# A mixture-of-experts kernel: y scatters in pairs, gathers on ACT's queue, 2 KB weight rows, and a plan in three parts

## The chip, the cores and the metric
One core of a Trainium2 chip runs the program. The metric is the device time in microseconds, the median of three runs. The profiled execution is one more run of the same kernel, read from its trace. TensorE is PE in the profile, VectorE DVE, ScalarE ACT, GpSimd POOL, SyncE SP.

## The reference
Float32 throughout; x is (32, 112, 256), the context (32, 375, 192).

```
x = x + xattn(layernorm(x), ctx)              # 8 heads of 64, softmax(q k') v, Wout, bout
x = x + ffn(layernorm(x))

def ffn(x):                                    # 3584 tokens, D 256, H 512, 8 experts, 2 of them per token
    logits = x @ Wr / sqrt(256)
    idx = top_k(logits + rb, 2)
    w = softmax(logits[idx])
    routed = sum over the two: w * (((x @ W1[e]) * silu(x @ W3[e])) @ W2[e])
    shared = ((x @ Ws1) * silu(x @ Ws3)) @ Ws2
    return routed + shared
```

## The kernel before
Matrices are split into a high and a low part, and a product is made from three matmuls, so weights exist as hi and lo halves.

**Attention** (`attention`, up to about 733 us) goes over 16 pairs of batch rows. Beside it the experts' weights are loaded half an expert at a time, split, and written to `wsplit` in DRAM: 16 halves, each `[128, 3072]` floats, so one row of 12 KB for each partition (`store_half`). W3, W1 and W2 with their lo parts make six `PIECES` of 512 columns.

**Experts** (`experts`) is a software pipeline over steps g: 28 shared steps ("S", one tile of 128 tokens each, with weights that lie in SBUF), then 63 routed steps ("R", one block j of 128 rows of one expert each). In step g TensorE does the up matmuls of g (`up3`, `up1`), the transposes of the hidden of g-1 (`turn`), the transposes of block g-26 (`turn_block`) and the down matmuls of g-1 (`down`). ACT does the scaled copy of y of g-2 (`copy_y`, L1238, into one of three `y_sb`), the Silu of g, the high part of the hidden of g-1 and that of block g-26 (`xr_hi`). VectorE does the addition of the shared y of g-2 into `acc` (`add_y`, L1453), the low part of g-1, the product (`hid`), and the low part of the block. Every engine works through its list in order and waits on semaphores.

While the shared steps run, the tokens are routed, in chunks of 512: VectorE finds the two experts, TensorE ranks the tokens in each (L1601 on), and GpSimd scatters each row with its token number and share to `x_sorted_scratch`, sorted by expert. After the last chunk, in step 19, VectorE makes the whole plan in one go (`make_plan`, L1374 to L1407): for each of the 63 blocks its expert, first row, place of its weights in the ring, and which of its rows lie outside. The rest of VectorE's step 20 stands behind it. SP then writes zeros behind each expert's last row (`padded`), for which it needs `row_end` from the plan.

In the routed stage:
- SP fills a ring of three slots with an expert's weights, two DMAs of 1536 KB each (`fill`, L1080). Slot 2 lies over `acc`, so fill 2 waits until all shared results are stored to `z_scratch` in DRAM. Fill e > 2 waits for the last down matmul of expert e-3.
- GpSimd loads block j's rows from `x_sorted_scratch` into one of four `xg` (`gather`, L1177), five blocks ahead, and adds y to its tokens' rows in `z_scratch` with an indirect accumulating DMA (`scatter_y`, L1186). Two experts may add to the same token, and two accumulates of one row must not be in flight together, so scatter j waits until scatter j-1 has landed. Rows outside the expert go to 128 dump rows behind the tokens.
- After the last scatter SP copies `z_scratch` to the output.

Of the kernel before, what the change touches and what calls it, by code (L numbers as in the profile page):

```python
# [10 lines left out]
F32 = mybir.dt.float32  # L11
F32R = mybir.dt.float32r
U32 = mybir.dt.uint32
# [7 lines left out]
def wait(eng, sem, count):  # L21

    if not isinstance(count, int) or count > 0:
        eng.wait_ge(sem, count)
# [110 lines left out]
def build(nc, x, ctx, Wq, Wk, Wv, Wout, bout, Wr, rb, W1, W2, W3, Ws1, Ws2, Ws3, out):  # L135
# [20 lines left out]
    PIECES = 6  # L156
# [9 lines left out]
    z_dram = nc.dram_tensor("z_scratch", (TOKENS + 128, D), F32, kind="Internal").ap()  # L166

# [44 lines left out]
def attention(nc, g):  # L212
# [15 lines left out]
    with own:  # L228
# [117 lines left out]
        def _(sp):  # L346
# [596 lines left out]
def experts(nc, g):  # L943
# [17 lines left out]
    SLOT = PIECES * 1024  # L961
    AHEAD = 5
    ROUND = 12582912.0
# [4 lines left out]
    with own:  # L968
# [35 lines left out]
        most, total, total_inv = sb("most", [128, TC]), sb("total", [128, TC]), sb("total_inv", [128, TC])  # L1004
        euler, dump_p = sb("euler", [128, 2, TC]), sb("dump_p", [128, 1])

# [33 lines left out]
        scattered = [sem(f"scattered{i}") for i in range(3)]  # L1040
        counts_made, plan, plan_ready = sem("counts_made"), sem("plan"), sem("plan_ready")
        chosen_ready, chosen_exp, shares_ready = sem("chosen_ready"), sem("chosen_exp"), sem("shares_ready")
# [6 lines left out]
        xr_made, xr_hi_ready, xr_ready = sem("xr_made"), sem("xr_hi_ready"), sem("xr_ready")  # L1049
        y_out = [sem(f"y_out{i}") for i in range(3)]  # L1050
        ring_in, zero_ready, padded = sem("ring_in"), sem("zero_ready"), sem("padded")
# [16 lines left out]
        def _(sp):  # L1068
# [21 lines left out]
            sp.wait_ge(zero_ready, 1)  # L1090
            sp.dma_start(z_dram[TOKENS:TOKENS + 128, :], zero_row[:, 0:D]).then_inc(z_stored, 16)
# [8 lines left out]
            sp.wait_ge(z_stored, 16 * (CHUNKS + 1))  # L1100
            for e in range(2, E):
# [5 lines left out]
            for i in range(3):  # L1107
                sp.wait_ge(y_out[i], 16 * ((BLOCKS - i + 2) // 3))
            whole = lambda t: t.rearrange("n d -> (n d)").rearrange("(p f) -> p f", p=128)
# [4 lines left out]
        def _(pool):  # L1114
# [7 lines left out]
                      allow_small_or_imprecise_dtypes=True)  # L1122
            pool.iota(dump_p[:], pattern=[[0, 1]], base=TOKENS, channel_multiplier=1,
                      allow_small_or_imprecise_dtypes=True)
# [82 lines left out]
            pool.wait_ge(plan_ready, 1)  # L1207
            pool.wait_ge(padded, 16 * E)
            for i in range(3):
                pool.wait_ge(scattered[i], 16 * 2 * TC * ((CHUNKS + 2 - i) // 3))  # L1210
            for j in range(AHEAD):
                gather(j)
            for j in range(BLOCKS):
                if j + AHEAD < BLOCKS:
                    gather(j + AHEAD)
                scatter_y(j)

        @block.scalar
        def _(act):
# [12 lines left out]
            def copy_y(g):  # L1232

                j = STEPS[g][1]
                act.wait_ge(y_made, g + 1)
                wait(act, y_out[j % 3], 16 * (j // 3))
                act.wait_ge(to_row_ready, j + 1)
                act.activation(y_sb[j % 3], YB[:, 0:D], ACT.Copy, scale=share[:, j:j + 1]).then_inc(y_copied, 1)  # L1238
# [36 lines left out]
            for g in range(LAST + 2):  # L1275
# [7 lines left out]
                if 0 <= j < BLOCKS:  # L1283
                    hi_of_block(j)
                if g < SHARED_FIRST:
                    c, at_step = (g + 2) // 3, g % 3
                    if at_step == 0 and c + 1 < CHUNKS:
                        normed(c + 1)
                    if at_step == 1 and 1 <= c < CHUNKS:
                        hi_of_x(c)  # L1290

        @block.vector
        def _(dve):
# [76 lines left out]

            def make_plan():

                dve.wait_ge(counts_made, 1)
                linked(dve.tensor_copy(count[:], XB[0][:, 0:E]))  # L1374
                linked(dve.tensor_scalar(blocks_f[:], count[:], 1.0 / BLOCK, 0.498, ALU.mult, ALU.add))
                linked(dve.tensor_scalar(blocks_f[:], blocks_f[:], ROUND, None, ALU.add))
# [6 lines left out]
                dve.tensor_copy(table_rows[:, 2, 0:1], count[:, 0:1])  # L1383
                dve.tensor_tensor(table_rows[:, 2, 1:E], count[:, 1:E], count[:, 0:E - 1], ALU.subtract)
# [6 lines left out]
                linked(last)  # L1391
                dve.tensor_reduce(expert1[:], past[:], AX.X, ALU.add)
                for n in range(3):
                    last = dve.tensor_reduce(of_block[:, n, :], past_of[:, n], AX.X, ALU.add)
                linked(last)
                dve.tensor_scalar(last_row[:], blocks_f[:, E - 1:E], float(BLOCK), float((E - 1) * CAP - BLOCK),
                                  ALU.mult, ALU.add)
                dve.tensor_tensor(row_end[:], count[:], base_e[:], ALU.add)
                dve.tensor_scalar(ring_at[:], of_block[:, 0, :], float(SLOT), None, ALU.mult)
# [6 lines left out]
                dve.tensor_scalar(from_row[:], row_f[:], last_row[:, 0:1], None, ALU.min)  # L1406
                dve.tensor_scalar(outside[:], left[:], iota_p[:, 0:1], dump_p[:, 0:1], ALU.is_le,  # L1407
                                  ALU.mult).then_inc(plan_ready, 1)

# [48 lines left out]
            for g in range(LAST + 2):  # L1458
# [10 lines left out]
                if g < SHARED_FIRST:  # L1469
# [193 lines left out]
```

## Time and profile before
| | before |
|---|---|
| median of 3 runs | 1270.85 us (1267.88 to 1272.77) |
| profiled execution, time | 1277.05 us |
| its span | 1275.4 us |
| mean granted TensorE clock | 0.957 |
| TensorE busy | 1165.7 us, 91% |
| VectorE busy | 748.1 us, 59% |
| ScalarE busy | 671.6 us, 53% |
| GpSimd busy | 802.0 us, 63% |

Times in the profile count from the span's start; the granted clock is 1.00 at 2.4 GHz and 0.50 at 1.2 GHz. An engine's busy share is a mean over stages with different limits, so stretches and waits have to be read as well. A timeline row gives start and duration, the engine and line, output<-inputs with their shapes, and in brackets how long the engine was idle before it and on whom it waited.

### The profile page before, as it was taken

What the parts mean: (1) busy time and instruction counts of PE and PEld (TensorE: products, weight loads), DVE (VectorE), ACT (ScalarE), POOL (GpSimd) and SP (SyncE); (2) the same over time, 40 slices, a digit from 0 to 9 for tenths busy, and PEclk for the clock granted to TensorE, in tenths of its full rate; (3) what the DMA queues carried; (4) which work ended last, traced back from release to release, by engine and by line L of the source; (5) the groups of instructions that cost most, each with busy time, mean ns of one, the idle gap of its engine ahead of it and who ended that gap; (6) DMA issues with size and microseconds to landing.
All of it is one profiled execution on the core that took longest, in us unless ns stands there. A gap on an engine that the chain in (4) does not pass through costs nothing. (4 is left out here: it accounts for less than half of the span.)

```text
span 1275.4 us, 27342 instructions
## 1 busy us (share of the span) xinstructions
PE 1165.7 (91%) x7710; PEld 1014.8 (80%) x7710; DVE 748.1 (59%) x2147; ACT 671.6 (53%) x1743; POOL 802.0 (63%) x867
## 2 busy tenths in 40 slices
PE   5989999999999999999998789996989999999792
PEld 4778888888888888888887678885878888888582
DVE  4667787778777877777777456565433333343231
ACT  4667776777677767776775342331233343433240
POOL 4778977897789778977897435654124444443241
PEclk9989999999999999999999689997999999999796
DMA  4213132213221322132214282212163354336634
GB/s 128 82 38 104 51 120 92 96 51 120 92 97 51 120 91 97 51 120 89 99 32 155 79 315 93 104 64 105 50 240 59 55 129 82 56 58 188 196 52 132
DMA packets 77104, 128.47 MB, mean 101 GB/s; under 512 B 18816, under 2 KB 63696, under 8 KB 72880
## 3 DMA queue, kind: packets, MB, share of 16 engines
q1 hardware_dynamic: 62256, 102.80, 23.9%
q0 software_dynamic: 14784, 24.84, 9.7%
q8 instruction: 37, 0.61, 0.2%
q14 instruction: 27, 0.22, 0.1%
HBM read 77.81 MB, written 53.48 MB: 103 GB/s over the span
## 5 line engine op out<-in xcount | busy, mean ns | idle before, releaser
L513 POOL TENSOR_TENSOR probs<-probs,inv_sum 112x375 f32<-112x375 f32 x256 | 208.9, 817 | 97.6 <-DVE inv_sum L742 97.6
L1186 POOL DMA_INDIRECT z_scratch<-stage,to_row x63 | 100.8, 1599 | 202.9 <-DMA z_scratch<-stage,to_row 102.6
L600 ACT ACTIVATE probs<-bank,neg_max 112x375 f32<-112x375 f32 x256 | 147.2, 575 | 126.7 <-DVE neg_max L730 123.5
L1432 DVE TENSOR_TENSOR hT_lo<-bank,hT_hi 128x512 fp32r<-128x512 f32 x91 | 62.9, 691 | 236.9 <-ACT hT_hi L1230 231.0
L730 DVE TENSOR_REDUCE neg_max<-bank 112x1 f32<-112x375 f32 x256 | 127.7, 541 | 32.5 <-PE bank L878 32.1
L907 PE MATMUL bank<-ident,probs 112*125 112x112 f32 x768 | 138.8, 291 | 7.7 <-POOL probs L513 7.7
L757 DVE TENSOR_TENSOR pT_lo<-bank,pT_hi 125x336 fp32r<-125x336 f32 x256 | 129.5, 506 | 27.1 <-ACT pT_hi L615 20.7
L907 PEld LDWEIGHTS bank<-ident,probs 112*125 112x125 f32 x768 | 107.2, 191 | 42.5 <-issue 24.4
L1224 ACT ACTIVATE stage<-bank 128x512 f32<-128x512 f32 x91 | 54.4, 598 | 154.9 <-PE bank L1496 152.7
L479 POOL TENSOR_TENSOR v_lo<-v_raw,v_hi 125x512 fp32r<-125x512 f32 x96 | 123.5, 1287 | 7.5
L615 ACT ACTIVATE pT_hi<-bank 125x336 fp32r<-125x336 f32 x256 | 113.4, 443 | 12.8 <-PE bank L907 12.8
L796 PE MATMUL bank<-pT_hi,v_hi 125*128 125x224 f32 x384 | 110.4, 287 | 2.0 <-DVE pT_lo L757 2.0
L476 POOL TENSOR_TENSOR v_hi<-v_raw,one 125x512 fp32r<-125x512 f32 x96 | 100.1, 1043 | 13.8 <-ACT v_raw L577 13.8
L796 PE MATMUL bank<-pT_hi,v_lo 125*128 125x224 f32 x384 | 106.7, 278 | 0.0
L1494 PE MATMUL bank<-ring,xr_hi 128*128 x252 | 106.3, 422 | 0.1
L796 PE MATMUL bank<-pT_lo,v_hi 125*128 125x224 f32 x384 | 106.1, 276 | 0.0
L1495 PE MATMUL bank<-ring,xr_hi 128*128 x252 | 100.0, 397 | 0.0
L1496 PE MATMUL bank<-ring,xr_lo 128*128 x252 | 100.0, 397 | 0.0
L742 DVE RECIPROCAL inv_sum<-row_sum 112x1 f32<-112x1 f32 x256 | 41.2, 161 | 92.8 <-ACT probs L600 92.7
L1177 POOL DMA_DIRECT2D xg<-x_sorted_scratch x63 | 66.7, 1059 | 33.3 <-issue 33.3
L688 DVE TENSOR_TENSOR k_lo<-bank,k_hi 128x376 fp32r<-128x376 f32 x128 | 69.3, 543 | 24.7 <-ACT k_hi L574 24.7
L1555 PE MATMUL bank<-ring,hT_hi 128*128 x504 | 78.2, 299 | 1.8 <-issue 1.0
(263 smaller groups left out, 3400.6 us busy)
## 6 DMA issues: line engine op xcount, KB each, us to landing
w_split_scratch<-stage SPq DMA_DIRECT2D x16, 1536.0 KB, 5.7
ring<-w_split_scratch SPq DMA_DIRECT2D x16, 1536.0 KB
stage<-in_L_ffn_W SPq DMA_DIRECT2D x48, 256.0 KB, 3.1
ctx_in<-in_ctx SPq DMA_DIRECT2D x32, 281.2 KB
xg<-x_sorted_scratch POOLq DMA_DIRECT2D x63, 136.0 KB, 3.5
x_in<-in_x SPq DMA_DIRECT2D x16, 224.0 KB, 4.0
x_res<-in_x SPq DMA_DIRECT2D x32, 112.0 KB, 3.1
x_scratch<-x SPq DMA_DIRECT2D x32, 112.0 KB, 1.9
```

The lines of the kernel that those rows point to most:

```text
L476: pool.tensor_tensor(v_hi[b][:, t, :], v_raw[at_v][:], one[0:KR, :].to_broadcast([KR, INNER]), ALU.mult).then_inc(v_hi_ready, 1)
L479: pool.tensor_tensor(v_lo[b][:, t, :], v_raw[at_v][:], v_hi[b][:, t, :].bitcast(F32), ALU.subtract).then_inc(v_ready, 1)
L513: pool.tensor_tensor(probs[:, s % 4, :], probs[:, s % 4, :], inv_sum[:, s:s + 1].to_broadcast([N, M]), ALU.mult).then_inc(probs_ready, 1)
L600: act.activation(probs[:, s % 4, :], S_BANK[s % 2][0:N, 0:M], ACT.Exp, bias=neg_max[:, s:s + 1], accum_out=row_sum[:, s:s + 1]).then_inc(e ...
L615: act.activation(pT_hi[:, (t // 2) % 2, :, t % 2, :], PT_BANK[t % 2][0:KR, 0:KT * N].rearrange("p (t n) -> p t n", t=KT), ACT.Copy).then_i ...
L730: dve.tensor_reduce(neg_max[:, s + n:s + n + 1], S_BANK[n][0:N, 0:M], AX.X, ALU.max, negate=True).then_inc(max_ready, 1)
L757: dve.tensor_tensor(pT_lo[:, (t // 2) % 2, :, t % 2, :], PT_BANK[t % 2][0:KR, 0:KT * N].rearrange("p (t n) -> p t n", t=KT), pT_hi[:, (t / ...
L796: mm = pe.matmul(o, lhsT, rhs, start=(n == 0), stop=(n == len(pairs) - 1))
L907: mm = pe.transpose(PT_BANK[t % 2][0:KR, kt * N:(kt + 1) * N], probs[:, t % 4, kt * KR:(kt + 1) * KR], ident[0:N, 0:N])
L1186: pool.indirect_dma_start(out=z_dram[:, :], out_offset=bass.IndirectOffsetOnAxis(ap=to_row[:, j:j + 1], axis=0), in_=y_sb[j % 3], in_offse ...
L1494: pe.matmul(o, hi, whi, start=(k == 0), stop=False)
L1495: pe.matmul(o, hi, wlo, start=False, stop=False)
```

## The change
- **Scatters.** `y_out` has two semaphores by turns. Scatter j waits for scatter j-2, and for j-1 only where j is the first block of an expert: the plan holds in `must_land[j]` to what value the other semaphore must have come. Two blocks in flight use different sets of dump rows (256 in all). There are four `y_sb`.
- **Gathers.** They move from GpSimd's queue to ACT's, four blocks ahead: gather j stands at the end of ACT's step j+24, behind `xr_hi` of block j-2. What the first gather waits for (the plan, the padding, the scattered rows) moves to ACT with it.
- **Weight rows.** `wsplit` becomes `(16, 6, 128, 512)`: stores and fills move 768 rows of 2 KB each in place of 128 of 12 KB.
- **Plan.** `make_plan` of step 19 becomes `plan_experts` (step 20, ending the wait of SP's padding early through `ends_ready`), `plan_blocks` (step 21), and `plan_sums` with `plan_rows` (step 22). `plan_rows` has two operations more, for `must_land`. Fill 2 waits for the plan as well.

```
-    wsplit = nc.dram_tensor("w_split_scratch", (HALVES, 128, 3072), F32, kind="Internal").ap()
+    wsplit = nc.dram_tensor("w_split_scratch", (HALVES, PIECES, 128, 512), F32, kind="Internal").ap()
...
-                sp.dma_start(wsplit[bass.ds(h, 1), :, :].rearrange("o p n -> p (o n)"),
-                             stage[:, 0:3072]).then_inc(stage_free, 16)
+                sp.dma_start(wsplit[bass.ds(h, 1), :, :, :].rearrange("o m p n -> p (o m) n"),
+                             stage[:, 0:3072].rearrange("p (m n) -> p m n", m=PIECES)).then_inc(stage_free, 16)
...
-    AHEAD = 5
+    AHEAD = 4
...
+        y_sb.append(sb("y_sb3", [128, D])[:])
...
-                    sp.dma_start(ring[:, cols].bitcast(F32), wsplit[2 * e + k]).then_inc(ring_in, 16)
+                    sp.dma_start(ring[:, cols].bitcast(F32).rearrange("p (m n) -> p m n", m=PIECES),
+                                 wsplit[2 * e + k].rearrange("m p n -> p m n")).then_inc(ring_in, 16)
...
-            sp.wait_ge(plan_ready, 1)
+            sp.wait_ge(ends_ready, 1)
             for e in range(E):
                 end = sp.value_load(row_end[0:1, e:e + 1], min_val=0, max_val=E * CAP - BLOCK)
...
-            def gather(j):
-                if j >= 4:
-                    pool.wait_ge(xr_made, j - 3)
-                    pool.wait_ge(to_row_ready, j - 3)
-                row = pool.value_load(from_row[0:1, j:j + 1], min_val=0, max_val=E * CAP - BLOCK)
-                pool.dma_start(xg[j % 4][:], xs_dram[bass.ds(row, BLOCK), :]).then_inc(xg_in[j % 4], 16)
...
             def scatter_y(j):
-                pool.wait_ge(y_copied, j + 1)
+                if 1 <= j < 3:
+                    pool.wait_ge(y_out[(j - 1) % 2], 16)
+                elif j >= 3:
+                    pool.wait_ge(y_out[(j - 1) % 2],
+                                 pool.value_load(must_land[0:1, j:j + 1], min_val=16, max_val=16 * BLOCKS))
+                    pool.sem_inc(landed, 1)
+                if j >= 2:
+                    pool.wait_ge(y_out[j % 2], 16 * (j // 2))
                 if j == 0:
                     pool.wait_ge(z_stored, 16 * (CHUNKS + 1))
-                else:
-                    pool.wait_ge(y_out[(j - 1) % 3], 16 * ((j - 1) // 3 + 1))
+                pool.wait_ge(y_copied, j + 1)
                 pool.indirect_dma_start(
                     out=z_dram[:, :], out_offset=bass.IndirectOffsetOnAxis(ap=to_row[:, j:j + 1], axis=0),
-                    in_=y_sb[j % 3], in_offset=None, compute_op=ALU.add).then_inc(y_out[j % 3], 16)
+                    in_=y_sb[j % 4], in_offset=None, compute_op=ALU.add).then_inc(y_out[j % 2], 16)
...
+            def gather(j):
+                if j == 0:
+                    act.wait_ge(plan_ready, 1)
+                    act.wait_ge(padded, 16 * E)
+                    for i in range(3):
+                        act.wait_ge(scattered[i], 16 * 2 * TC * ((CHUNKS + 2 - i) // 3))
+                if j >= 4:
+                    act.wait_ge(xr_made, j - 3)
+                    act.wait_ge(to_row_ready, j - 3)
+                row = act.value_load(from_row[0:1, j:j + 1], min_val=0, max_val=E * CAP - BLOCK)
+                act.dma_start(xg[j % 4][:], xs_dram[bass.ds(row, BLOCK), :]).then_inc(xg_in[j % 4], 16)
...
+                linked(dve.scalar_tensor_tensor(must_f[:, 1:BLOCKS], within[:, 1:BLOCKS], 0.0, earlier[:, 0:BLOCKS - 1],
+                                                ALU.is_le, ALU.add))
+                dve.tensor_scalar(must_land[:, 1:BLOCKS], must_f[:, 1:BLOCKS], 16.0, None, ALU.mult)
...
-                        if g == RANK_STEPS[-1]:
-                            make_plan()
+                    if g == RANK_STEPS[-1] + 1:
+                        plan_experts()
+                    if g == RANK_STEPS[-1] + 2:
+                        plan_blocks()
+                    if g == RANK_STEPS[-1] + 3:
+                        plan_sums()
+                        plan_rows()
```

## Rows read from the trace of the kernel before

**Rows 1.** busy time by stretch (length, engines, granted clock, DMA share, GB/s)
```profile
811.00:821.00 10.00, 9.45 (x57) 8.45 (x57) 7.06 (x26) 3.24 (x7) 5.58 (x8) 0.83 0.04 15
881.50:887.40 5.90, 5.84 (x23) 5.18 (x24) 1.53 (x3) 0.34 (x1) 1.93 (x2) 0.54 0.46 165
950.00:956.45 6.45, 1.57 (x7) 0.68 (x5) 1.38 (x2) 0.29 (x2) 1.40 (x2) 0.90 0.49 181
956.45:962.70 6.25, 6.25 (x24) 5.52 (x25) 0.55 (x3) 1.47 (x4) 3.03 (x4) 0.56 0.39 52
1058.00:1155.00 97.00, 96.88 (x596) 84.44 (x596) 35.45 (x98) 38.49 (x79) 44.97 (x42) 1.00 0.36 59
1164.00:1172.00 8.00, 8.00 (x52) 6.96 (x50) 3.69 (x10) 3.15 (x7) 2.21 (x2) 1.00 1.00 395
1180.00:1186.40 6.40, 0.85 (x4) 0.37 (x2) 1.38 (x2) 0.14 (x1) 0.00 (x0) 0.80 0.82 302
```

**Rows 2.** ACT line L1238, then the timeline: start, duration, instruction
```profile
L1238 ACT ACTIVATE stage<-bank,share x63: 474/474/479, 928.2 to 1253.3; 128x256 f32<-128x256 f32 x63
...
1118.47 0.47 ACT L1238 ACTIVATE stage<-bank,share 128x256 f32<-128x256 f32 x1 [1.05 <-PE bank L1558]
...
1123.34 0.47 ACT L1238 ACTIVATE stage<-bank,share 128x256 f32<-128x256 f32 x1 [1.04 <-PE bank L1558]
1124.73 0.60 ACT L1224 ACTIVATE stage<-bank 128x512 f32<-128x512 f32 x1 [0.92 <-PE bank L1496]
```

**Rows 3.** waits of TensorE, 925 to 1256: total us, times, longest
```profile
PE bank L1568 <- DMA xg<-x_sorted_scratch: 14.3, 4, 5.7
```

**Rows 4.** chain that ended last: start, us, what
```profile
928.95 8.48 DMA z_scratch<-stage,to_row
...
938.20 3.96 DMA z_scratch<-stage,to_row
...
943.99 11.57 DMA xg<-x_sorted_scratch
```

**Rows 5.** timelines of DVE and PE around the plan
```profile
872.67 0.16 DVE L1374 COPY count<-bank 128x8 f32<-128x8 f32 x1
...
874.20 0.68 DVE L1385 TENSOR_TENSOR past<-iota_j,blocks_up 128x504 f32<-128x504 f32 x1
...
876.85 0.68 DVE L1392 TENSOR_REDUCE expert<-past 128x63 f32<-128x504 f32 x1
...
880.78 0.31 DVE L1407 TENSOR_SCALAR outside<-left,iota_p,dump_p 128x63 uint32<-128x63 f32 x1
...
881.56 1.19 PE L1555 MATMUL bank<-w_hi,hT_hi 128*128 128x256 f32 x4 [10.66 <-DVE ring L1453]
```

**Rows 6.** timelines of DVE and PE, an undisturbed shared step
```profile
893.56 0.69 DVE L1427 TENSOR_TENSOR hid<-bank,stage 128x512 f32<-128x512 f32 x1
...
897.91 0.63 PE L1555 MATMUL bank<-w_hi,hT_hi 128*128 128x256 f32 x4
```

**Rows 7.** SP timeline; then the page: KB each, us to landing
```profile
733.68 6.86 SPq L1075 DMA_DIRECT2D ring<-x_scratch  x7
...
882.07 8.69 SPq L1097 DMA_DIRECT2D x_sorted_scratch<-zero_row  x8
...
942.81 0.80 SPq L1080 DMA_DIRECT2D ring<-w_split_scratch  x2
...
xg<-x_sorted_scratch POOLq DMA_DIRECT2D x63, 136.0 KB, 3.5
```

**Rows 8.** DMA queues from 929 to 937.4: packets, MB, share of 16 engines
```profile
q1 hardware_dynamic: 264, 2.85, 80.7%
q0 software_dynamic: 192, 0.27, 14.3%
```

**Rows 9.** timeline of POOL, the last two scatters
```profile
1253.15 1.55 POOL L1186 DMA_INDIRECT z_scratch<-stage,to_row  x1 [2.96 <-DMA z_scratch<-stage,to_row]
1257.76 1.55 POOL L1186 DMA_INDIRECT z_scratch<-stage,to_row  x1 [3.06 <-DMA z_scratch<-stage,to_row]
```

More of the change, by code:

```diff
@@ L162, in build @@
     HALVES = 2 * E
-    wsplit = nc.dram_tensor("w_split_scratch", (HALVES, 128, 3072), F32, kind="Internal").ap()
+    wsplit = nc.dram_tensor("w_split_scratch", (HALVES, PIECES, 128, 512), F32, kind="Internal").ap()
     ROW, CAP = 272, TOKENS + 128
     xs_dram = nc.dram_tensor("x_sorted_scratch", (E * CAP, ROW), F32, kind="Internal").ap()
-    z_dram = nc.dram_tensor("z_scratch", (TOKENS + 128, D), F32, kind="Internal").ap()
+    z_dram = nc.dram_tensor("z_scratch", (TOKENS + 256, D), F32, kind="Internal").ap()
     top = ExitStack()
@@ L1040, in experts @@
         scattered = [sem(f"scattered{i}") for i in range(3)]
-        counts_made, plan, plan_ready = sem("counts_made"), sem("plan"), sem("plan_ready")
+        counts_made, ends_ready, plan_ready = sem("counts_made"), sem("ends_ready"), sem("plan_ready")
         chosen_ready, chosen_exp, shares_ready = sem("chosen_ready"), sem("chosen_exp"), sem("shares_ready")
@@ L1049, in experts @@
         xr_made, xr_hi_ready, xr_ready = sem("xr_made"), sem("xr_hi_ready"), sem("xr_ready")
-        y_out = [sem(f"y_out{i}") for i in range(3)]
+        landed, y_out = sem("landed"), [sem(f"y_out{i}") for i in range(2)]
         ring_in, zero_ready, padded = sem("ring_in"), sem("zero_ready"), sem("padded")
@@ L1100, in _ @@
             sp.wait_ge(z_stored, 16 * (CHUNKS + 1))
+            sp.wait_ge(plan_ready, 1)
             for e in range(2, E):
@@ L1105, in _ @@
                 fill(e)
-            for i in range(3):
-                sp.wait_ge(y_out[i], 16 * ((BLOCKS - i + 2) // 3))
+            for i in range(2):
+                sp.wait_ge(y_out[i], 16 * ((BLOCKS - i + 1) // 2))
             whole = lambda t: t.rearrange("n d -> (n d)").rearrange("(p f) -> p f", p=128)
@@ L1122, in _ @@
                       allow_small_or_imprecise_dtypes=True)
-            pool.iota(dump_p[:], pattern=[[0, 1]], base=TOKENS, channel_multiplier=1,
+            pool.iota(dump[:], pattern=[[0, (BLOCKS + 1) // 2], [128, 2]], base=TOKENS, channel_multiplier=1,
+                      allow_small_or_imprecise_dtypes=True)
+            pool.iota(earlier[:], pattern=[[1, (BLOCKS + 1) // 2], [0, 2]], base=0, channel_multiplier=0,
                       allow_small_or_imprecise_dtypes=True)
@@ L1207, in _ @@
             pool.wait_ge(plan_ready, 1)
[L1208 to L1212, printed above, removed]
             for j in range(BLOCKS):
-                if j + AHEAD < BLOCKS:
-                    gather(j + AHEAD)
                 scatter_y(j)
@@ L1235, in copy_y @@
                 act.wait_ge(y_made, g + 1)
-                wait(act, y_out[j % 3], 16 * (j // 3))
+                wait(act, y_out[j % 2], 16 * (j // 2 - 1))
                 act.wait_ge(to_row_ready, j + 1)
-                act.activation(y_sb[j % 3], YB[:, 0:D], ACT.Copy, scale=share[:, j:j + 1]).then_inc(y_copied, 1)
+                act.activation(y_sb[j % 4], YB[:, 0:D], ACT.Copy, scale=share[:, j:j + 1]).then_inc(y_copied, 1)
             def hi_of_block(j):
@@ L1284, in _ @@
                     hi_of_block(j)
+                if 0 <= g + AHEAD - SHARED_FIRST < BLOCKS:
+                    gather(g + AHEAD - SHARED_FIRST)
                 if g < SHARED_FIRST:
@@ L1369, in take_slots, with plan_experts @@
                 dve.tensor_copy(slot_u[:, :, ts], slot_f[:]).then_inc(slots_ready, 1)
-            def make_plan():
+            def plan_experts():
                 dve.wait_ge(counts_made, 1)
                 linked(dve.tensor_copy(count[:], XB[0][:, 0:E]))
+                dve.tensor_tensor(row_end[:], count[:], base_e[:], ALU.add).then_inc(ends_ready, 1)
                 linked(dve.tensor_scalar(blocks_f[:], count[:], 1.0 / BLOCK, 0.498, ALU.mult, ALU.add))
@@ L1383, in make_plan, with plan_blocks @@
                 dve.tensor_copy(table_rows[:, 2, 0:1], count[:, 0:1])
-                dve.tensor_tensor(table_rows[:, 2, 1:E], count[:, 1:E], count[:, 0:E - 1], ALU.subtract)
+                last = dve.tensor_tensor(table_rows[:, 2, 1:E], count[:, 1:E], count[:, 0:E - 1], ALU.subtract)
+                linked(last)
+            def plan_blocks():
                 linked(dve.tensor_tensor(past[:], iota_j[:].rearrange("p (j o) -> p j o", o=1).to_broadcast([128, BLOCKS, E]),
@@ L1391, in make_plan, with plan_sums @@
                 linked(last)
+            def plan_sums():
                 dve.tensor_reduce(expert1[:], past[:], AX.X, ALU.add)
@@ L1395, in make_plan, with plan_rows @@
                 linked(last)
+            def plan_rows():
                 dve.tensor_scalar(last_row[:], blocks_f[:, E - 1:E], float(BLOCK), float((E - 1) * CAP - BLOCK),
                                   ALU.mult, ALU.add)
-                dve.tensor_tensor(row_end[:], count[:], base_e[:], ALU.add)
                 dve.tensor_scalar(ring_at[:], of_block[:, 0, :], float(SLOT), None, ALU.mult)
@@ L1406, in make_plan @@
                 dve.tensor_scalar(from_row[:], row_f[:], last_row[:, 0:1], None, ALU.min)
-                dve.tensor_scalar(outside[:], left[:], iota_p[:, 0:1], dump_p[:, 0:1], ALU.is_le,
-                                  ALU.mult).then_inc(plan_ready, 1)
+                linked(dve.scalar_tensor_tensor(must_f[:, 1:BLOCKS], within[:, 1:BLOCKS], 0.0, earlier[:, 0:BLOCKS - 1],
+                                                ALU.is_le, ALU.add))
+                dve.tensor_scalar(must_land[:, 1:BLOCKS], must_f[:, 1:BLOCKS], 16.0, None, ALU.mult)
+                dve.scalar_tensor_tensor(outside[:], left[:], iota_p[:, 0:1], dump[:, 0:BLOCKS], ALU.is_le,
+                                         ALU.mult).then_inc(plan_ready, 1)
             def take_chosen(c):
```

7 lines of the change are left out of this document (5 added, 2 removed).

## The prediction
> **What bounds the kernel now.** I read the page first, then the busy time by stretch, the waits, the chain, and the timelines around each gap. Attention (up to 733 us) is touched only in how the split weights are stored, so the question is which gaps TensorE has after it. Between 1058 and 1155 it has none (96.88 of 97 us busy) and its granted clock is 1.00 [rows 1]. From 950 to 956.45 it is busy 1.57 of 6.45 us, and then works 6.25 us at a clock of 0.56, nearly all at the lower level (1.2 GHz); from 1180 to 1186.4 it is busy 0.85 of 6.4, with the same behind it, and a third gap of this kind, half as long, follows at about 1199 [rows 1]. Where it is not disturbed, then, the routed stage is bound by matmuls: one block in 4.87 us [rows 2].
>
> The causes. In the routed stage TensorE waited 14.3 us on L1568, in four waits, for gathered blocks (xg) [rows 3]. The chain shows why those were late: with a fill of the weight ring just issued, a y scatter took 8.48 us to land against 3.96 without one, and a gather issued right behind a scatter 11.57 us [rows 4]. GpSimd waits for scatter j-1 to land before it issues scatter j, and every gather stands in that same queue. A longer gap before the routed stage is another matter: TensorE waited 10.66 us, until 881.56, for an addition on VectorE (L1453), which stood behind the plan of the blocks [rows 5]; and then worked 5.84 us at 0.54 [rows 1].
>
> The first copy of y starts at 928.2 and the last at 1253.3 [rows 2], 325.1 us apart; 62 undisturbed steps are 62 x 4.87 = 302.0. So 23.1 us are lost in the routed stage, stalls and lower clock together. The first gap explains 4.9 idle and 6.25/2 = 3.1 of lost speed, 8.0; the second 5.55 and as much speed, 8.7; the third, half as long, the rest.
>
> **The change, part by part.**
>
> *The plan in three parts.* The plan runs on VectorE from 872.67 to about 881.0 (its last operation starts at 880.78) [rows 5]. Moved behind the next three steps, it leaves VectorE free at about 872.7, the addition ends at 873.1 and TensorE starts at about 873.2 rather than 881.56: 8.3 us less. The lower clock cost 5.84/2 = 2.9 us after that gap. But a stretch with only 0.55 us idle, 811 to 821, also has a mean clock of 0.83, which costs 0.17 x 10 = 1.7 [rows 1]; so I expect 1.7 to stay: 1.2 less.
> What the parts cost where they go: in an undisturbed shared step VectorE is free from 894.2 until the addition, which must end by 897.9 [rows 6]: 897.9 - 0.15 - 0.4 - 894.2 = 3.15 us. The first part takes 1.6 us (872.67 to 874.2) and the second 2.65 (874.20 to 876.85): hidden, with 0.5 to spare; without that cover they would cost their own length. The third takes 4.15 (876.85 to 881.0) plus two operations more on 63 columns (such a one, outside, is busy 0.31; they overlap a little): 0.45, together 4.6, over by 1.45. TensorE waits that long once, and half-speed time may follow: 1.7 again, which I count. Net: 8.3 + 1.2 - 1.45 - 1.7 = 6.4. Bounds: 2 if the second part overflows too, 9.5 if no half-speed time follows.
> The row ends come first, so SP's eight padding writes (8.69 us [rows 7]) start about 6 us sooner, at 876, and have landed by about 888; the first gather, now at step 24, comes at about 893. It does not wait.
>
> *Gathers on ACT's queue.* Per block ACT gets a register load and a DMA; the same pair takes SP 8.69/8 = 1.09 us [rows 7]. Behind it in ACT's order stand the copy of y, the Silu and the copy of hT. In an undisturbed step ACT is idle 1.04 us before the copy of y and 0.92 before the Silu [rows 2]: 1.96 us free between xr_hi and the Silu. So 1.09 is hidden; above 1.96 the Silu comes late, and at the latest once TensorE's own slack is used up each further microsecond is paid in every block. Cost 0.
> The gather is issued up to 1.5 us after the transposes of block j-2 and needed two steps after them, less the 0.3 of the transposes themselves: 9.74 - 0.3 - 1.5 = 7.9 us. Alone a gather lands in 3.5 us [rows 7] (the median on POOL; none on ACT is in the trace). Its cover is 4.4 us. It no longer stands behind a scatter or behind one's landing.
>
> *2 KB weight rows.* A fill moves two times 1536 KB at 395 GB/s with its engines fully busy [rows 1], so about 8 us, and one of 16 engines moves 12 KB in 12288/24.7 GB/s = 0.50 us. The scatter under a fill took 4.5 us longer for 8 rows per engine, 0.57 for each: as if each row let one 12 KB piece pass. In 929 to 937.4 both queues' packets are indeed mixed (264 beside 192) [rows 8]. With 2 KB pieces it is 8 x 0.083 = 0.7 us for a scatter and as much for a gather, 1.4 when both are in flight. Gather under a fill: 3.5 + 1.4 = 4.9, under 7.9. Fills themselves may take longer (768 pieces each); but a slot is refilled when its expert is done and needed two experts later, so some twenty us early even at experts of two blocks: up to double is hidden. For the sixteen stores in attention only SP waits. I count 0, bound 2.
>
> *Two scatters in flight, four y buffers.* GpSimd's turn is now 1.6 us of issue, and before it register loads and starting: the last scatters lie 4.6 us apart [rows 9], some 3.9 of it the landing (3.96 in [rows 4]), so 0.7, with one load more perhaps 1.2. That is 2.8, under 4.87, so it follows ACT's copies. It waits for a landing only at an expert's first block; 3.9 to 5.3 us of landing against 4.87 between copies costs at most about a microsecond there, caught up at once and waited for by nobody (four buffers). Routed stage: 23.1 less; bounds 17 (one gap stays) and 23.1. I take 22.9.
>
> *The end.* The last copy of y starts at 1253.3, the last scatter only at 1257.76, because it waits for the one before [rows 2, 9]. It will follow the copy's end (1253.8) by about 0.3: 1257.76 - 1253.8 - 0.3 = 3.7; I take 3.5 (bounds 2.5 and 3.7). The copy of the output to its place stays.
>
> **Sum**: 6.4 + 22.9 + 3.5 = 32.8 us. The profiled execution: span 1275.4, time 1277.05, so 1.65 around it; it becomes 1242.6 and 1244.2. That execution was 6.2 above the median of 1270.85; the median becomes 1238.1.
>
> **Rivals.**
> *B, the fills still hold up the gathers,* now because both go through hardware descriptor generation. For it: seven issues with 1 KB rows took SP 6.86 us, 0.98 each, a fill issue with 12 KB rows 0.80/2 = 0.40 [rows 7]; more pieces, more issue time. By that, 1536 pieces take 2.9 us, and a gather behind them lands in 4.9 + 2.9 = 7.8, just in time. If it has to wait for the whole fill, 8 + 3.5 = 11.5, 3.6 late, and some 3 of lower clock behind: 6.6 for each fill that a gather falls behind. Fills start at the end of a down matmul, about when the gather is issued, so between none and five: at three, 20 us, 1258. Against it: the queues' packets mix now.
> The Trainium skill ("DMA: Bandwidth & Descriptors", section on queues, rings and completion order) says that SP's and ACT's queues have a ring of their own on each of the same engines, but no descriptor generator of their own. That is rival B's mechanism; no row of before has a DMA on ACT, so the trace can neither confirm nor refuse it.
> *C, slower than before: ACT becomes the bound.* If load and issue occupy ACT for c us per block, TensorE pays up to (c - 1.96) x 61 steps. The gain of 32.8 is gone at c = 2.5; at 3.0 the time is 1238 + 63 = 1301. For it: ACT's Silu and hT copy feed every step. Against it: 1.09 on SP.
> *D, the three parts only move the stall:* plan_rows and the lower clock take all of the first term: 1238 + 6.4 = 1244.5.
>
> **Chances**: forecast 0.74, B 0.14, D 0.07, C 0.05. The forecast's own range is 1233 to 1247, from the terms' bounds. 1231 to 1253 takes in D and the milder half of B, and leaves 0.14 or so outside. Faster by over 0.5% (about 6 us, what a measurement of this kernel can tell): forecast, D and most of B, 0.92; within: 0.03; slower: C, and B at its worst, 0.05.
>
> **What the profile would show.** TensorE: a gap of 2 to 3 us near 871 instead of 10.66, one of about 1.5 two or three steps on; none over 1 us in the routed stage, clock 1.00 there; copies of y 4.87 us apart throughout, 302 us from first to last; no wait of L1568 for xg. Gathers under 7.9 us to landing, scatters under a fill 5 to 6. GpSimd waiting for ACT's copies. The last scatter under 0.5 us behind the last copy. Wrong if: gathers land late beside fills (B), ACT idle for no time before the Silu (C), or the second gap is as long as the first (D).

## The result

The change made the kernel faster: a median of 1238.97 us in four runs (1236.79 to 1243.91) against 1271.22 (1267.88 to 1272.77) before it, also in four, one more than in the table of before, a ratio of 0.9755 (95% interval 0.972 to 0.979). The prediction was 1238.1, range 1231 to 1253. The profiled execution took 1238.53 us with a span of 1236.8.

The waits of TensorE after 900 us in the changed kernel (total us, times, longest) are down to one line; the 14.3 us of [rows 3] are gone:
```profile
PE bank L1587 <- ACT hT_hi L1229: 0.8, 1, 0.8
```

Busy time by stretch (columns as in [rows 1]):
```profile
868.50:873.00 4.50, 4.50 (x21) 3.95 (x21) 2.31 (x14) 0.38 (x1) 3.59 (x4) 0.62 0.43 150
880.00:888.00 8.00, 7.02 (x35) 6.07 (x36) 7.07 (x22) 2.12 (x4) 0.00 (x0) 0.79 0.30 102
888.00:910.00 22.00, 22.00 (x137) 19.20 (x136) 8.79 (x20) 5.88 (x12) 0.00 (x0) 1.00 0.17 51
913.00:1216.00 303.00, 302.68 (x1859) 263.80 (x1857) 113.58 (x305) 120.04 (x247) 95.22 (x61) 1.00 0.51 119
```
The last row is the routed stage: 303 us, in which TensorE is busy for 302.68, at a granted clock of 1.00. There is nothing left there but matmuls. The first two rows are the neighbourhood of the plan, where 1.2 GHz stretches remain (0.62 and 0.79).

The scaled copies of y on ACT (duration min/median/max in ns, then first and last start), in two groups because the fourth buffer has a name of its own:
```profile
L1237 ACT ACTIVATE stage<-bank,share x48: 474/474/479, 917.6 to 1218.3; 128x256 f32<-128x256 f32 x48
L1237 ACT ACTIVATE y_sb<-bank,share x15: 474/477/477, 932.2 to 1206.0; 128x256 f32<-128x256 f32 x15
```
From first to last 1218.3 - 917.6 = 300.7 us, against 325.1 in [rows 2].

What was one gap of 10.66 us in [rows 5] is now this, in the timelines of VectorE and TensorE (start, duration, instruction, idle time before it and what ended it):
```profile
868.97 0.15 DVE L1388 COPY count<-bank 128x8 f32<-128x8 f32 x1
...
875.12 0.67 DVE L1404 TENSOR_TENSOR past<-iota_j,blocks_up 128x504 f32<-128x504 f32 x1
879.84 0.42 DVE L1480 TENSOR_TENSOR ring<-ring,bank 128x256 f32<-128x256 f32 x1 [2.15 <-remote]
882.16 0.67 DVE L1414 TENSOR_REDUCE expert<-past 128x63 f32<-128x504 f32 x1
...
886.24 0.28 DVE L1434 SCALAR_TENSOR_TENSOR outside<-left,iota_p,dump 128x63 uint32<-128x63 f32 x1
```
```profile
868.00 0.71 PE L1587 MATMUL bank<-w_hi,hT_hi 128*128 128x256 f32 x4 [2.33 <-DVE ring L1480]
...
874.25 0.63 PE L1587 MATMUL bank<-w_hi,hT_hi 128*128 128x256 f32 x4
...
880.98 0.74 PE L1587 MATMUL bank<-w_hi,hT_hi 128*128 128x256 f32 x4 [1.92 <-ACT hT_hi L1229]
...
887.28 0.64 PE L1587 MATMUL bank<-w_hi,hT_hi 128*128 128x256 f32 x4
```
The three parts of the plan start at 868.97, 875.12 and 882.16, a step apart. TensorE waits 2.33 us before the first of these down matmuls, not 10.66. The wait of 1.92 before 880.98 is one that I had not foreseen: VectorE was idle for 2.15 us before its addition at 879.84, and ACT stood too. The profile puts this wait to "remote", which means another core or an unknown queue.

The end, in GpSimd's timeline (compare [rows 9]):
```profile
1216.61 1.56 POOL L1192 DMA_INDIRECT z_scratch<-stage,to_row  x1 [2.40 <-DMA z_scratch<-stage,to_row]
1219.53 1.56 POOL L1192 DMA_INDIRECT z_scratch<-stage,to_row  x1 [1.37 <-ACT stage L1237]
```
The last scatter waits for the last copy (1218.3) and no longer for the scatter before it: it starts 1.2 us behind the copy's start, where it was 1257.76 - 1253.3 = 4.5.

### The profile page after: what moved, and what is told of

It is laid out like the page before. It is cut to its first block and busy times, and to the rows that moved or that the text cites. A ratio compares the mean times of both kernels' runs of the same rounds, so it can differ in the third digit from the quotient of the medians.

```text
span 1236.8 us, 27587 instructions
## 1 busy us (share of the span) xinstructions
PE 1153.5 (93%) x7710; PEld 1007.3 (81%) x7710; DVE 746.6 (60%) x2149; ACT 671.3 (54%) x1743; POOL 762.1 (62%) x805
## 5 line engine op out<-in xcount | busy, mean ns | idle before, releaser
L1192 POOL DMA_INDIRECT z_scratch<-stage,to_row x48 | 75.0, 1562 | 187.5 <-ACT stage L1237 141.2
L730 DVE TENSOR_REDUCE neg_max<-bank 112x1 f32<-112x375 f32 x256 | 127.7, 540 | 32.7 <-PE bank L878 32.3
L688 DVE TENSOR_TENSOR k_lo<-bank,k_hi 128x376 fp32r<-128x376 f32 x128 | 69.2, 541 | 24.7 <-ACT k_hi L574 24.6
L796 PEld LDWEIGHTS bank<-pT_hi,v_hi 125*128 125x128 f32 x384 | 74.4, 194 | 2.5 <-DVE pT_lo L757 2.5
L1587 PE MATMUL bank<-ring,hT_hi 128*128 x504 | 75.6, 292 | 0.8 <-ACT hT_hi L1229 0.8
```

The source lines that it names most:

```text
L730: dve.tensor_reduce(neg_max[:, s + n:s + n + 1], S_BANK[n][0:N, 0:M], AX.X, ALU.max, negate=True).then_inc(max_ready, 1)
L796: mm = pe.matmul(o, lhsT, rhs, start=(n == 0), stop=(n == len(pairs) - 1))
L1587: pe.matmul(YB[:, 0:D], hT_hi[g % 2][:, m, :], ws[m][n], start=(m == 0 and n == 0), stop=False)
```

## The experiments

**How they were read.** The u kernels ran on one chip, the v kernels on another, the w kernels on a third, and the kernel before was timed on each of them (medians 1258.28, 1260.11 and 1269.92 us). "First pair" means the two kernels of the result. Ratios are compared within a chip; they are the recorded ones, and the quotient of two medians can differ from them by 0.1% or so. From one profile of each kernel I read four lengths, each from the first or last start of a line: S, from the first to the last conversion of slots (slot_u), shared stage before the plan, the same code in every kernel; A, from there to the first copy of y, with the plan in it; B, from the first to the last copy of y; C, from the last copy to the last scatter. S and A differ between chips for the same kernel (A is 50.2 and 46.1 for the changed one), C hardly. B agrees to within 0.3 us for the changed kernel (300.7 and 300.4), but for an untouched routed stage it is 325.1 in the kernel before and 321.3 in v2, so differences from it are uncertain by some 4 us.

| kernel | chip | median us | ratio (95%) | S | A | B | C |
|---|---|---|---|---|---|---|---|
| before | first pair | 1271.22 | | 115.7 | 55.6 | 325.1 | 4.5 |
| after | first pair | 1238.97 | 0.9755 (0.972 to 0.979) | 111.2 | 50.2 | 300.7 | 1.2 |
| u1 plan whole | u | 1231.66 | 0.9794 (0.9775 to 0.9813) | 98.8 | 56.0 | 300.2 | 1.2 |
| u2 12 KB rows | u | 1230.48 | 0.9781 (0.9759 to 0.9803) | 98.8 | 46.0 | 309.4 | 1.3 |
| u3 serial scatters | u | 1228.64 | 0.9777 (0.9756 to 0.9798) | 98.8 | 46.1 | 300.7 | 9.4 |
| u4 gathers on GpSimd | u | 1223.91 | 0.9739 (0.9717 to 0.976) | 98.8 | 46.0 | 303.1 | 1.2 |
| v1 after | v | 1222.40 | 0.9688 (0.9659 to 0.9717) | 100.3 | 46.1 | 300.4 | 1.2 |
| v2 plan alone | v | 1248.07 | 0.9902 (0.9873 to 0.9931) | 99.7 | 45.8 | 321.3 | 5.0 |
| v3 rows alone | v | 1252.28 | 0.9925 (0.9896 to 0.9955) | 98.8 | 55.5 | 316.1 | 5.4 |
| v4 plan in four | v | 1220.72 | 0.9683 (0.9653 to 0.9713) | 98.7 | 44.9 | 300.0 | 1.2 |
| w1 gathers on ACT alone | w | 1272.49 | 1.0011 (0.9984 to 1.0038) | 112.8 | 55.3 | 324.6 | 10.2 |
| w2 pairs alone | w | 1263.56 | 0.995 (0.9918 to 0.9982) | 107.6 | 56.1 | 321.3 | 1.2 |
| w3 ACT held longer | w | 1248.77 | 0.9832 (0.9788 to 0.9876) | 112.1 | 51.7 | 310.4 | 1.2 |
| w4 1 KB rows | w | 1238.05 | 0.9742 (0.9701 to 0.9783) | 113.5 | 51.4 | 300.0 | 1.2 |

The first four undo one part of the change each.

**u1: the plan in one piece.**
```
-                    if g == RANK_STEPS[-1] + 1:
+                    if g == RANK_STEPS[-1]:
                         plan_...
-                    if g == RANK_STEPS[-1] + 2:
-                    if g == RANK_STEPS[-1] + 3:
```


> The changed kernel with the plan again in one piece in step 19 (still with the two operations for must_land); scatters in pairs, gathers on ACT and 2 KB rows stay. My theory: TensorE gets its gap of some 10 us and the lower clock behind it back, the two short stalls of the three parts go: 5.4 to 6.4 us more than 1239, so 1244.5 to 1245.5. Rival D (the three parts only moved the stall): 1239.

Its A is 56.0 where the other three of its chip have 46.0 to 46.1: the three parts are worth 10.0 us there, where I had expected 5.4 to 6.4. B and C stay. The first row is of TensorE's timeline and shows the gap; the second is the stretch behind it (columns as above), at a granted clock of 0.57:
```profile
866.11 1.19 PE L1585 MATMUL bank<-w_hi,hT_hi 128*128 128x256 f32 x4 [9.33 <-DVE ring L1480]
```
```profile
866.00:872.00 6.00, 5.89 (x24) 5.28 (x25) 1.58 (x3) 0.53 (x2) 1.43 (x2) 0.57 0.53 187
```

**u2: weight rows of 12 KB again.**
```
-    wsplit = nc.dram_tensor("w_split_scratch", (HALVES, PIECES, 128, 512), F32, ...
+    wsplit = nc.dram_tensor("w_split_scratch", (HALVES, 128, 3072), F32, ...
```


> The changed kernel with 12 KB weight rows again. My theory: each row of a gather or scatter lets one 12 KB piece pass (0.50 us), so a gather under a fill lands in 3.5 + 4 = 7.5 us alone and up to 11 with a scatter in flight, against 7.9 of cover: a stall of 0 to 3 us, with lower clock behind it, at some of the six fills: 1241 to 1254. Rival R: what removed the stalls was only that gathers stand in a queue of their own: 1239, no wait of TensorE for xg.

B grows by 9.0 over the changed kernel's 300.4. TensorE waits for gathers again, but only 1.1 us in four waits; the two waits for hT_hi, 2.3 us, come from ACT, which stood 6.5 us before the copy of y until scatters had landed. No lower clock is in the 9.0, against my expectation: in 15 stretches of 20 us and one of 16, from 895 to 1211, it is 1.00 in each, and TensorE idles 5.8 us in all of them together. Four of the stretches, beside the first and the last fills, hold 4.8 of this and only 106 to 116 matmuls, where undisturbed ones hold 123 or more. This is the emptiest:
```profile
1135.00:1155.00 20.00, 18.43 (x106) 14.87 (x105) 7.12 (x18) 7.31 (x15) 1.56 (x2) 1.00 0.76 274
```
So the 9.0 us are lost beside the fills, but the waits account for only part of them; what the rest is stays open. Landing times of the scatters (L1191) in this kernel, min/median/max:
```profile
DMA to landing us min/median/max: 3.6/3.8/12.2
```

**u3: one scatter at a time, four buffers kept.**
```
-                if 1 <= j < 3:
-                    ...
+                if j >= 1:
+                    pool.wait_ge(y_out[(j - 1) % 2], 16 * ((j - 1) // 2 + 1))
```


> The changed kernel with one scatter in flight: scatter j waits until j-1 has landed. My theory: a scatter's round takes 4.6 us, under the 4.87 of TensorE's step, and nobody but the end waits for it, so only the end is later, by the lag GpSimd has piled up under the last fills: 3 to 4 us, 1242 to 1243. Rival S: the pairs are what removed the stalls, because late scatters hold the y buffers and ACT's copies: with them gone TensorE stalls at the fills again, 1250 or more.

B stays at 300.7, so within the routed stage nobody waits for the serial scatters when rows are 2 KB and there are four y buffers. But C is 9.4, more than the 4.5 of the kernel before and than the 3 to 4 us that I had expected. Under the last fills GpSimd waits up to 7.39 us for a landing, and the scatter of the copy that starts at 1162.36 comes 12.5 us behind it, at 1174.90. From there the scatters follow one another every 3.8 to 5.3 us against steps of 4.9, and TensorE has no stalls in which they could catch up more; at the last copy (1199.25) they are still 9.5 us behind. GpSimd's timeline, last two:
```profile
1204.97 1.56 POOL L1186 DMA_INDIRECT z_scratch<-stage,to_row  x1 [2.42 <-DMA z_scratch<-stage,to_row]
...
1208.72 1.56 POOL L1186 DMA_INDIRECT z_scratch<-stage,to_row  x1 [2.19 <-DMA z_scratch<-stage,to_row]
```

**u4: gathers back in GpSimd's queue** (ahead of each scatter, five blocks ahead, as before).


> The changed kernel with the gathers back in GpSimd's queue, five ahead, in front of each scatter; pairs and 2 KB rows stay. My theory: with no landing to wait for and 2 KB pieces the gathers are in time from GpSimd too (3.5 + 1.4 us under a fill, two steps of cover): 1239 to 1241. Rival Q: a gather has to stand outside GpSimd's queue, since there it waits for ACT's copies and for the first landings of each expert: gaps of several us at the fills, 1248 or more.

B is 303.1, 2.7 longer than v1's, with one wait of 0.8 us for a gather, so rival Q's gaps of several us aren't there. Once rows and pairs are in place, moving the gathers is worth about 2.7 us.

**v1: the changed kernel on another chip,** as the yardstick for v2 to v4.


> The changed kernel itself, as the base for these runs. The ratio of 0.9755 should come back; by the runs that undo one part (0.9794, 0.9781, 0.9777, 0.9739) it should be at or under 0.974. From the first to the last copy of y about 301 us, the last scatter under 1.5 us behind the last copy's start.

The ratio is 0.9688, a larger gain than the first pair's. A is 46.1, 4.1 less than in the first profile. TensorE's down matmuls around the plan:
```profile
857.07 0.71 PE L1587 MATMUL bank<-w_hi,hT_hi 128*128 128x256 f32 x4 [0.60 <-DVE ring L1480]
...
861.76 0.63 PE L1587 MATMUL bank<-w_hi,hT_hi 128*128 128x256 f32 x4
...
866.40 0.63 PE L1587 MATMUL bank<-w_hi,hT_hi 128*128 128x256 f32 x4
...
872.10 0.71 PE L1587 MATMUL bank<-w_hi,hT_hi 128*128 128x256 f32 x4 [0.89 <-DVE ring L1480]
```
An undisturbed step is 866.40 - 861.76 = 4.64; the one with the third part 5.70, so that part costs 1.06. No "remote" wait falls among them. Against it, the three steps from 868.00 to 887.28 in the first profile are 6.25, 6.73 and 6.30 us long: 1.6 more in the first (its granted clock is 0.73), 2.1 more in the second (the "remote" wait), and 1.66 more in the third. The third part of the plan lies in that last step too, but TensorE doesn't wait for it there: it is busy all the time, at a low clock:
```profile
880.98:887.28 6.30, 6.30 (x28) 5.36 (x29) 6.16 (x20) 1.20 (x2) 0.00 (x0) 0.73 0.37 127
```
A clock of 0.73 costs 0.27 x 6.30 = 1.7 us, the whole of the 1.66. So this is the price of the lower clock behind the "remote" gap, and the third part costs nothing visible in the first profile and 1.06 us, a wait at full clock, in v1.

**v2 and v3: one part alone, on the kernel before.**
```
 v2:                     if g == RANK_STEPS[-1] + 1:    (and + 2, + 3; nothing else)
 v3: +    wsplit = nc.dram_tensor("w_split_scratch", (HALVES, PIECES, 128, 512), F32, ...
```


> The kernel before with nothing changed but the plan in three parts. My theory: the parts lie behind matmuls but for some 1.5 us, so about 6.4 us less (ratio 0.995) by the terms of the prediction, up to 10 less by the start of the routed stage where the plan was put back in one piece (56.0 us from slot_u to the first copy of y against 46.0). Rival D: nothing (1.000).

> The kernel before with nothing changed but 2 KB weight rows. My theory: a gather behind a scatter under a fill passes two times 8 pieces of 0.083 us in place of 0.50, so the three gaps of TensorE (13.8 us) and the lower clock behind them go for the most part: 15 to 20 us less, ratio 0.985 to 0.988; the last scatter still waits for the one before. Rival R: the gathers are late since they stand behind the landing of the scatter before, whatever the rows: under 5 us less, 0.996 or more.

The plan alone saves 1.0%, more than the 0.5% of my terms; its A is as short as v1's. Rows alone save 0.75%, half of what I expected; B is 316.1, 5.2 less than v2's and 9.0 less than that of the kernel before. TensorE still waits for gathers in v3, shorter (compare [rows 3]); they still stand behind each scatter's landing there:
```profile
PE bank L1569 <- DMA xg<-x_sorted_scratch: 5.3, 4, 3.6
```

**v4: the plan in four parts,** the fourth a step later.
```
+                    if g == RANK_STEPS[-1] + 4:
```


> The changed kernel with the last part of the plan cut again: plan_sums in step 22, plan_rows in step 23. My theory: the third part of about 4.6 us passes the 3.15 that a shared step leaves VectorE, two of about 2.5 don't: one stall of 1.3 us and the lower clock behind it go, 1 to 3 us less than the changed kernel. Rival: the lower clock comes from the gap before the parts (about 2.3 us, when TensorE waits for slot_u) and not from the third, so under 1 us less.

The third part's wait is gone (A 44.9, 1.2 less). The ratio, 0.9683, is the lowest of all, but it can't be told from v1's 0.9688.

**w1: gathers on ACT alone.**


> The kernel before with nothing changed but the gathers on ACT's queue, four ahead. My theory now: a gather that is late in the kernel before stands behind a scatter and its landing, so a queue of its own removes most of the three gaps; what is left is what the 12 KB pieces cost beside it, 9 us from first to last copy of y, as where the 12 KB rows were put back (309.4 us). The lag of the serial scatters at the end grows to 9 us or so. From first to last copy about 310 us in place of some 321, but the end later: ratio 0.993 to 0.998. Rival: with serial scatters under 12 KB rows the y copies wait for their buffers and the gaps stay, 1.000.

No gain at all, as the rival had it. The waits of the whole core from 915 to 1260 (same columns as TensorE's) show why:
```profile
ACT stage L1223 <- DMA z_scratch<-stage,to_row: 39.4, 9, 10.5
...
PE bank L1555 <- ACT hT_hi L1215: 15.2, 5, 6.8
```
TensorE waits for a gather only once now, for 0.6 us. But the scatters are still serial and late under a fill, the three y buffers fill up, ACT stands up to 10.5 us before the copy of y, and TensorE waits 15.2 us for ACT in place of 14.3 for the gathers. Whether a fourth buffer alone would have been enough here was not tried: w2 and the changed kernel bring it together with the pairs.

**w2: pairs of scatters and four buffers alone** (gathers on GpSimd, 12 KB rows, whole plan).


> The kernel before with pairs of scatters and four y buffers alone: gathers in GpSimd's queue, 12 KB rows, the plan in one piece in step 19 (with the two operations for must_land). My theory: each expert's first scatter still waits for a landing under a fill, with the gathers behind it, but a gather waits for no other landing: first to last copy 308 to 314 us, the last scatter 1.2 us behind the last copy in place of 5; ratio 0.988 to 0.991. Rival: as long as gathers stand behind landings at the experts' borders, where the fills start, the gaps stay: 320 us and only the end is gained, 0.997.

C is 1.2, so the end is fixed. But B is 321.3, as long as v2's, whose routed stage is untouched, and not the 308 to 314 that I had expected: the rival was right. TensorE waits 11.2 us in three waits for gathers (L1597); in v2 it is 13.2 us in three.

**w3: ACT held longer.** Four copies of 128x272 behind each gather, each waited for, so that their results change nothing.
```
+                for k in range(4):
+                    act.activation(act_pad[:], zero_row[:], ACT.Copy).then_inc(pad_made, 1)
+                    act.wait_ge(pad_made, 4 * j + k + 1)
```


> The changed kernel with four copies of a [128, 272] tile of zeros on ACT behind each gather, each waited for before the next, some 0.5 us each: ACT is held c = 0.85 + 2.0 = 2.9 us per block between xr_hi and the copy of y. It measures where rival C would have begun. By the prediction's free time (1.96 us) the cost is up to 0.9 x 61 = 55 us; with the 0.6 to 0.7 us that TensorE's down matmuls leave behind the Silu it is 0.3 x 61 = 18 us. If even 2.9 us are hidden: 0.

ACT's timeline, first of the changed kernel, then of w3:
```profile
1062.38 0.39 ACT L1244 ACTIVATE xr_hi<-bank 128x256 fp32r<-128x256 f32 x1 [0.96 <-PE bank L1600]
1063.28 0.34 ACTq L1258 DMA_DIRECT2D xg<-x_sorted_scratch  x1
1063.80 0.47 ACT L1237 ACTIVATE stage<-bank,share 128x256 f32<-128x256 f32 x1 [1.04 <-PE bank L1590]
1065.19 0.60 ACT L1223 ACTIVATE stage<-bank 128x512 f32<-128x512 f32 x1 [0.92 <-PE bank L1528]
```
```profile
1064.24 0.39 ACT L1246 ACTIVATE xr_hi<-bank 128x256 fp32r<-128x256 f32 x1 [0.44 <-PE bank L1605]
1065.27 0.34 ACTq L1260 DMA_DIRECT2D xg<-x_sorted_scratch  x1
1065.66 1.82 ACT L1262 ACTIVATE act_pad<-zero_row 128x272 f32<-128x272 f32 x4 [1.03 <-DVE share L1477]
1067.51 0.47 ACT L1239 ACTIVATE stage<-bank,share 128x256 f32<-128x256 f32 x1
```
In the changed kernel load and issue end at 1063.28 + 0.34 = 1063.62, 0.85 after xr_hi, and ACT then still waits for TensorE before the copy of y. In w3 ACT is taken for 1067.51 - 1064.63 = 2.88 us, 0.92 more than the 1.96 that [rows 2] leave free. B is 10.0 longer, 0.16 us per step, not 0.92. Part of the difference shows in these rows: ACT was also idle for 0.96 us before xr_hi, which my 1.96 leave out, and in w3 this is 0.44. The rest I put down to slack that TensorE has between ACT's products and their use; no run measures it.

**w4: 1 KB rows** (12 pieces of 256 columns).


> The changed kernel with weight rows of 1 KB (12 pieces of 256 columns). My theory of one piece passed per row: under a fill a scatter and a gather would pass 0.04 us in place of 0.083, so the longest scatter landing falls from 8.8 to 7 us or less; but nothing waits for them any more, so the time stays within 0.2% of the changed kernel (0.967 to 0.971). Rival: what makes landings long under a fill is the engines' full load, not the size of the pieces; then they stay at 8 to 9 us, and 1536 pieces a fill make the fills longer still, with weights late at the two experts of two blocks: some us slower.

B is 300.0 against v1's 300.4, nothing more to gain. The ratio of 0.9742 misses the 0.967 to 0.971 that I had expected. The changed kernel itself didn't run on this chip, so the ratio can't show whether 1 KB rows help or harm; but A is 51.4 where v1 has 46.1, and those 5.3 us are 0.4% of the time, in a stretch that has nothing to do with the rows. Scatters (L1192) in v1 with 2 KB rows, then in w4 with 1 KB rows:
```profile
DMA to landing us min/median/max: 3.7/3.8/8.8
```
```profile
DMA to landing us min/median/max: 3.7/3.9/7.3
```

## Why the prediction was right

The two profiled executions lie 38.6 us apart in span, where the sum said 32.8. 5.2 of the 38.6 lie before the plan, in code that the change doesn't touch (S is 4.5 shorter, its start 0.7 earlier); the medians are 32.3 apart. The rest answers to the terms one by one:

| term | predicted | first profiles | what else the runs say |
|---|---|---|---|
| plan in three parts | 6.4 (2 to 9.5) | 55.6 - 50.2 = 5.4 | 10.0 on chip u, 9.7 between v2 and v3, 3.9 to 4.7 on chip w (w1 and w2 against w4) |
| routed stage | 22.9 (17 to 23.1) | 325.1 - 300.7 = 24.4 | 321.3 - 300.4 = 20.9 between v2 and v1 |
| end | 3.5 (2.5 to 3.7) | 4.5 - 1.2 = 3.3 | 4.2 between v3 and v1 |
| output copy | 0 | 0.3 | |

**The plan.** In the first profile the gap shrinks by 10.66 - 2.33 = 8.33, as predicted (8.3), and 1.6 of lower clock stay behind it (1.7 predicted). The third part, for which I had 1.45 + 1.7, costs nothing visible; but the "remote" wait, which I had not foreseen, takes 2.1 and the lower clock behind it 1.66. The 3.15 and the 3.8 nearly cancel, and that is luck. Between u1 and v1, where no such wait falls, the term that was mis-sized shows: 9.33 - 0.60 = 8.73 of gap and 873.10 - 866.11 - 4.64 = 2.35 of lower clock go, 1.06 comes back, 10.0 in all (A says 9.9). I had charged 1.7 of lower clock behind both small gaps, and neither had any there. My upper bound of 9.5 was added up wrong besides: 8.3 + 2.9 - 1.45 is 9.75, still under the 9.9. The range of 1233 to 1247 doesn't follow from the terms' bounds either, which give 1234.6 to 1249.4; 1238.97 lies in both. By the medians the same change saves 37.7 us on chip v, more than the upper bounds of all terms together (36.3), so it is partly luck that the first pair comes within 1 us of the sum. D, that the stall only moves, is refuted by v1, and v4 takes away even the moved 1.06.

**Routed stage.** The stalls and the lower clock behind them went, and B came out a little under the 302.0 of the sum (300.7), since the last three steps take only 4.66, 4.70 and 2.93 us. How much they had cost is less sure than it looked: B of an untouched routed stage is 325.1 in one profile and 321.3 in another. (The third gap of the prediction, for which [rows 1] has no row, is 3.35 us long and ends at 1202.04.) The undisturbed cover (7.9 us for a gather) was the right thing to compare with, but the fills were under-priced: the longest scatter under a fill took 8.8 us (I said 5 to 6) and the longest gather 7.9 in v1 (I said 4.9), the whole of its cover. That nothing stalled was thus closer than the prediction had it. The gathers' (L1258) landing times in v1:
```profile
DMA to landing us min/median/max: 2.0/2.1/7.9
```
Pieces matter in the direction that I gave: the longest scatter of a profile took 11.3 to 12.2 us with 12 KB rows (before, u2, v2, w1), 8.2 to 9.0 with 2 KB (seven profiles) and 7.3 with 1 KB (w4 alone). But going from 12 to 1 KB takes off 4.9 of the 8.4 us over the median. By my reading the rest is the engines' full load (share 1.00 in [rows 1]); no run tests that. The fills themselves take a little longer with small rows, 10.9 us to landing in the median in u2 and 11.7 in u3 on the same chip, and nobody waited for that. The Trainium skill ("DMA: Bandwidth & Descriptors", section on queues, rings and completion order) has each DMA engine take turns between its queues packet by packet; the runs agree as far as a small transfer's wait falls with the row size.

**Gathers on ACT** cost nothing, as said: 0.85 us of ACT against my 1.09 and the 1.96 free. B, that they'd wait for whole fills, is not seen: after 900 us TensorE never waits for a gather in either profile of the changed kernel. The longest gather took 7.9 us, though, as in B's mild form (7.8). Nothing speaks for B's reasons: in u4 the gathers came from GpSimd's queue instead and the longest took 8.4, no less, and a fill's issue took SP 0.54 us in the median (the longest of 16 took 2.17), so about 1.1 for 1536 pieces, not 2.9. C, ACT as the bound, had its price too high: w3 goes past the free time by 0.92 and pays 0.16 per step. Its threshold left out the 0.96 us before xr_hi; where each further microsecond would be paid in full, no run shows.

**Pairs and four buffers.** "Caught up at once and waited for by nobody" held (C 1.2; the last scatter starts 1219.53 - 1218.3 - 0.47 = 0.8 us behind the copy's end, where I had 0.3). What I didn't see is how little each part is worth by itself. Alone, over its own chip's kernel before: gathers on ACT 0, pairs 0.5%, rows 0.75%, plan 1.0%, together 2.2%; the whole change 3.1% in v1. Those of the routed stage cover for one another. Against the untouched 321.3 to 325.1, rows alone shorten B by 5.2 to 9.0, pairs by 0 to 3.8, gathers by 0.5 at most, and all three by 20.9 to 24.7. Undone alone, the price is 8.2 us at the end for the pairs, 9.0 for the rows, 2.7 for the gathers, 9.9 for the plan. Each of four estimates for the whole change on chip u, its run less its own price (u1: 1231.66 - 9.9, u2: 1230.48 - 9.1, u3: 1228.64 - 8.2, u4: 1223.91 - 2.7), over 1258.28 gives 0.970 to 0.971, like v1's quotient of medians, 1222.40/1260.11 = 0.970. Of the first pair's 0.9755, some 0.35% are the 4.5 us by which its plan term is smaller.

**Open.** What the "remote" waits are. The six profiles with an S over 107 all have some on ACT and VectorE in the shared stage, and the eight with an S near 99 have none. They are about as long as what S is longer by: VectorE's before `hid` come to 16.2 us in the kernel before, whose S is 16.9 over 98.8, and to 14.0 in w1, whose S is 14.0 over it. Where the plan is in three parts (the changed kernel's first profile, w3, w4) one of them also falls beside the plan, and the plan term is the smaller for it. The medians of the kernel before, 1270 to 1271 us against 1258 to 1260, go with it. Open too: how much the fourth y buffer does without the pairs.

## What to carry to other kernels

When a transfer is late because it stands behind another, list everything that the other one holds: w1 freed the gathers, and the same serial scatters stopped the kernel through its y buffers instead, for the same time. Small transfers beside a bulk one should meet small rows: going from 12 to 2 KB rows took 3.4 us off the worst scatter (u2 and v1), and 1 KB took off another 1.5 without shortening the routed stage. Work that isn't due for some steps belongs in the slack of those steps, cut to the slack's length; where it overflows, the overflow is all that is paid (1.06 us here), and no lower clock need follow.

## What the runs showed of the hardware

- The same 136 KB gather lands in a median of 2.1 us from ACT's queue and 3.5 from GpSimd's (v1 and u4; 3.5 in [rows 7] too). I had costed ACT's at 3.5.
- The same shared-stage code (S) took 98.7 to 100.3 us in all eight profiles on chips u and v, and 107.6 to 115.7 in the other six, the ones with "remote" waits. That is up to 17 us between profiles of untouched code, more than any single part of this change is worth; without S beside it, a difference of two single profiles would mislead.
- Whether a short gap of TensorE is followed by a stretch at 1.2 GHz differs, and the length of the gap alone doesn't tell: in the changed kernel's first profile the granted clock is 0.62 behind the gap of 2.33 us (868.5 to 873) and 0.50 from 883 to 885, behind the one of 1.92; but it is 1.00 behind a gap of 1.86 in w4 (870 to 874.5) and behind that of 0.60 in v1. The stretches behind these two, w4 and then v1:
```profile
870.00:874.50 4.50, 4.50 (x28) 3.96 (x29) 3.11 (x16) 1.09 (x2) 3.33 (x4) 1.00 0.33 112
857.00:861.70 4.70, 4.63 (x28) 4.14 (x29) 3.33 (x16) 1.09 (x2) 3.37 (x4) 1.00 0.32 111
```
